# Layer norm centring in two rounded passes, with ScalarE's half copies one step earlier

## The reference

```
for i in range(6):
    x = attention(shift_tokens(x)) + x      # 16 heads of 64, windows of 32 with the window before
    x = ffn(shift_tokens(x)) + x

shift_tokens(t): the first 64 channels as they are, the last 64 one token later (zero first)
attention: q, k, v = t @ Wqkv; q, k L2-normalised, scaled, rotated; softmax(8 q k') v; @ Wo
ffn: mu = mean(t); var = mean((t - mu)^2)
     xn = (t - mu) / sqrt(var + 1e-5) * g + b
     a, gate = split(xn @ W1 + b1); out = (a * gelu(gate)) @ W2 + b2
```

## Time and profile before

| | |
|---|---|
| median of 3 runs | 1684.48 us (1683.54 to 1689.99) |
| the profiled execution | 1684.45 us, its span 1682.7 us |
| PE busy | 1569.3 us (93%) |
| DVE busy | 1448.3 us (86%) |
| ACT busy | 1116.0 us (66%) |
| POOL busy | 1071.4 us (64%) |

### The profile page before, as it was taken

How to read it: one execution, slowest core, us unless ns; L and a number is a source line. 1 busy time by engine, 2 the same in 40 slices (tenths; PEclk the granted TensorE clock), 3 DMA queues, 4 the chain that set the end, 5 groups by cost and what they waited for, 6 DMA issues and landing times.

```text
span 1682.7 us, 77735 instructions
## 1 busy us (share of the span) xinstructions
PE 1569.3 (93%) x33167; PEld 1272.7 (76%) x33168; DVE 1448.3 (86%) x3173; ACT 1116.0 (66%) x2014; POOL 1071.4 (64%) x1040
## 2 busy tenths in 40 slices
PE   4469999999999999999999999999999999999987
PEld 2247878778878878888878787778788878887874
DVE  8969989889889988889988889889899888888862
ACT  4336677667677667677667676767766766776753
POOL 4656767675676666667667567576577585675640
PEclk7679999999999999999999999999999999999999
DMA  2011111211111211111211111211111111111010
GB/s 88 32 55 41 41 38 43 74 35 40 36 47 38 60 44 49 33 51 29 69 33 51 42 38 41 63 37 53 42 38 41 56 44 49 30 45 53 25 47 14
DMA packets 41086, 75.09 MB, mean 45 GB/s; under 512 B 9472, under 2 KB 22568, under 8 KB 40744
## 3 DMA queue, kind: packets, MB, share of 16 engines
q1 hardware_dynamic: 40744, 70.12, 14.4%
HBM read 20.08 MB, written 2.10 MB: 13 GB/s over the span
## 4 chain that ended last, share of the span: by engine, by line
PE 72%; issue 8%; DVE 7%; ACT 4%; POOL 4%; ACTq 0%; DVEq 0%; POOLq 0%
PE bank L1372 8%; PE bank L1340 8%; PE bank L1423 7%; PE bank L1497 7%; PE wide L1465 7%; PE bank L1342 6%; PE bank L1341 6%; PE bank L1482 5%; PE bank L1562 4%; PE bank L1442 3%; PE bank L1411 2%; PE bank L1547 2%; POOL qk L864 2%; PE bank L1548 1%; PE bank L1549 1%
## 5 line engine op out<-in xcount | busy, mean ns | idle before, releaser
L872 POOL TENSOR_TENSOR qk<-qk,rnorm 128x512 f32<-128x512 f32 x384 | 402.2, 1048 | 346.9 <-DVE rnorm L1025 346.9
L864 POOL TENSOR_TENSOR qk<-qk,qk_sin 128x512 f32<-128x512 f32 x384 | 492.7, 1283 | 144.3 <-DVE qk_sin L986 144.3
L1188 ACT ACTIVATE squares<-bank 128x512 f32<-128x512 f32 x384 | 229.7, 598 | 152.2 <-DVE qk_sin L986 152.2
L996 DVE TENSOR_REDUCE norm<-squares 128x8 f32<-128x512 f32 x384 | 258.0, 677 | 30.7 <-ACT squares L1188 28.5
L1340 PE MATMUL bank<-w_hi,xs_hi 128*128 128x512 f32 x576 | 263.3, 457 | 11.8 <-ACT squares L1188 6.6
L979 DVE TENSOR_TENSOR qk<-bank,tables 128x512 f32<-128x512 f32 x384 | 261.2, 680 | 7.3 <-PE bank L1342 7.1
L986 DVE TENSOR_TENSOR qk_sin<-bank,tables 128x512 f32<-128x512 f32 x384 | 260.8, 679 | 0.6 <-POOL qk L864 0.6
L1372 PE MATMUL bank<-ident,qk 128*128 128x128 f32 x1536 | 225.2, 277 | 4.9 <-POOL qk L872 4.1
L1342 PE MATMUL bank<-w_hi,xs_lo 128*128 128x512 f32 x576 | 228.2, 396 | 0.0
L1341 PE MATMUL bank<-w_lo,xs_hi 128*128 128x512 f32 x576 | 227.2, 394 | 0.7 <-issue 0.7
L1372 PEld LDWEIGHTS bank<-ident,qk 128*128 128x128 f32 x1536 | 180.5, 141 | 42.7 <-POOL qk L872 4.9
(11 more groups left out here) (181 smaller groups left out, 2738.7 us busy)
## 6 DMA issues: line engine op xcount, KB each, us to landing
v<-v SPq DMA_DIRECT2D x96, 390.0 KB, 3.5
v<-v SPq DMA_DIRECT2D x72, 130.0 KB, 3.5
w_raw<-in_L_ffn_Wqkv SPq DMA_DIRECT2D x36, 256.0 KB, 3.1
w_o_s<-in_L_ffn_Wo SPq DMA_DIRECT2D x6, 512.0 KB, 4.0
w_raw<-in_L_ffn_W SPq DMA_DIRECT2D x6, 341.0 KB, 3.4
mix_x_nat<-in_L_attn_x SPq DMA_DIRECT2D x4, 256.0 KB, 3.2
w_raw<-x_res_scratch SPq DMA_DIRECT2D x4, 256.0 KB, 3.3
out<-w_raw SPq DMA_DIRECT2D x4, 256.0 KB, 3.1
```

Source lines behind the costliest of these rows:

```text
L864: pool.tensor_tensor(qk[:, g % 2, c, :], qk[:, g % 2, c, :], qk_sin[:, (QK_CHUNKS * g + c) % SINES, :], ALU.add).then_inc(added[c], 1)
L872: pool.tensor_tensor(view, view, rnorm[:, g % 2, c * HPC:(c + 1) * HPC].unsqueeze(2) .to_broadcast([P, HPC, DH]), ALU.mult).then_inc(norme ...
L996: dve.tensor_reduce(norm2[:, c * HPC:(c + 1) * HPC], squares[:, c % 2, :].rearrange("p (h d) -> p h d", d=DH), AX.X, ALU.add).then_inc(sum ...
```

## The change

`centre` becomes two passes with rounded operands: `center_r` times `xs2_hi`, and later `center_r` times `xs2_lo`, summed in bank 5. `center_r` is a rounded copy of `center`, made once by DVE. `xs2_hi` is made by ACT (`round_tail`), `xs2_lo` by POOL (`split_tail`); they use the memory of `xn_hi` and `xn_lo`. The half copies leave the start of `t == 3`: the first (`take_tail`) stands in step `t == 2` behind `take_probs`, the second (`shift_tail`) in the same step behind `square(step, 3)`. `lo_ready` takes the place of `xn_ready` and counts both low parts. Three small tensors of the root become slices of one.

```
@@ constants and tensors
-    N_CONST = 9
+    N_CONST = 10
-        norm2, root_t, root_w = (sb(name, [P, NORMS + NBLK]) for name in ("norm2", "root_t", "root_w"))
+        norms = sb("norms", [P, 3, NORMS + NBLK])
+        norm2, root_t, root_w = (norms[:, n, :] for n in range(3))
+        xs2_hi, xs2_lo = xn_hi, xn_lo
+        center_r = sb("center_r", [P, P], F32R)
-        xn_ready, gelu_done = sem("xn_ready"), sem("gelu_done")
+        lo_ready, gelu_done = sem("lo_ready"), sem("gelu_done")
@@ POOL
             def split_xn(m):
-                ....then_inc(xn_ready, 1)
+                ....then_inc(lo_ready, 1)
+            def split_tail(m):
+                if not real(m):
+                    return
+                pool.wait_ge(xs2_ready, 3 * (m + 1))
+                pool.tensor_tensor(xs2_lo[:], xs2[:], xs2_hi[:].bitcast(F32), ALU.subtract).then_inc(lo_ready, 1)
             def add_first_residual(m):
-                pool.wait_ge(xs2_ready, 2 * (m + 1))
+                pool.wait_ge(xs2_ready, 3 * (m + 1))
@@ POOL, in each step
+                if t == 3:
+                    split_tail(item - 1)
                 normalise(step - 1, 3)
                 add(step - 1, 2)
@@ DVE, once
+            dve.tensor_scalar(center_r[:], center[:], 1.0, 0.0, ALU.mult, ALU.add).then_inc(constants_ready, 1)
             dve.wait_ge(constants_ready, N_CONST)
@@ ACT
+            def take_tail(m):
+                if not real(m):
+                    return
+                act.wait_ge(x1_done, NBLK * (m + 1))
+                need(act, lo_ready, 2 * m - 1)
+                act.copy(xs2[0:half, :], x1[0:half, m % 2, :]).then_inc(xs2_ready, 1)
             def shift_tail(m):
-                act.wait_ge(x1_done, NBLK * (m + 1))
-                need(act, centred, m)
-                act.copy(xs2[0:half, :], x1[0:half, m % 2, :]).then_inc(xs2_ready, 1)
                 act.copy(xs2[half:P, 1:SEQ], x1[half:P, m % 2, 0:SEQ - 1]).then_inc(xs2_ready, 1)
+            def round_tail(m):
+                if not real(m):
+                    return
+                act.wait_ge(xs2_ready, 3 * m + 2)
+                need(act, up_ready, NHID * m)
+                act.copy(xs2_hi[:], xs2[:]).then_inc(xs2_ready, 1)
@@ ACT, in each step
                 if t == 3:
-                    shift_tail(item - 1)
+                    round_tail(item - 1)
                 take_v(step, 0)
                 take_qk(step - 2, 0)
@@
                 take_probs(step - 2, 0)
                 take_probs(step - 2, 1)
                 if t == 2:
+                    take_tail(item - 1)
                     take_out(item - 2)
                 if t == 0:
                     gelu(item - 2, 0)
                 square(step, 3)
+                if t == 2:
+                    shift_tail(item - 1)
                 take_qk(step - 1, 2)
                 take_v(step, 1)
@@ PE
             def centre(m):
-                pe.wait_ge(xs2_ready, 2 * (m + 1))
+                pe.wait_ge(xs2_ready, 3 * (m + 1))
-                pe.matmul(bank[5][:], center[:], xs2[:], start=True, stop=True).then_inc(centred, 1)
+                pe.matmul(bank[5][:], center_r[:], xs2_hi[:], start=True, stop=False)
+            def centre_rest(m):
+                if not real(m):
+                    return
+                pe.wait_ge(lo_ready, 2 * m + 1)
+                pe.matmul(bank[5][:], center_r[:], xs2_lo[:], start=False, stop=True).then_inc(centred, 1)
             def expand(m, j):
-                    pe.wait_ge(xn_ready, m + 1)
+                    pe.wait_ge(lo_ready, 2 * m + 2)
@@ PE, in each step
                 weigh(step - 3, 1)
+                if t == 3:
+                    centre_rest(item - 1)
```

More of the change, by code:

```diff
@@ L878, in split_xn @@
                 pool.wait_ge(xn_copied, 2 * (m + 1))
-                pool.tensor_tensor(xn_lo[:], xn[:], xn_hi[:].bitcast(F32), ALU.subtract).then_inc(xn_ready, 1)
+                pool.tensor_tensor(xn_lo[:], xn[:], xn_hi[:].bitcast(F32), ALU.subtract).then_inc(lo_ready, 1)
+            def split_tail(m):
[3 more added lines that the diff above has]
+                pool.tensor_tensor(xs2_lo[:], xs2[:], xs2_hi[:].bitcast(F32), ALU.subtract).then_inc(lo_ready, 1)
             def add_first_residual(m):
```

## The result

| | before | after |
|---|---|---|
| median (4 runs each) | 1685.8 us (1683.54 to 1689.99) | 1714.35 us (1704.67 to 1717.62) |
| ratio, with 95% interval | | 1.0158 [1.0136, 1.0181] |
| profiled execution, its span | 1684.45 us, 1682.7 us | 1716.12 us, 1714.3 us |

The kernel became 1.6% slower. The forecast was 1704 us with a range of 1682 to 1711, so the direction was right and the time lies 3 us above the range. The two profiled executions differ by 31.7 us; the sum had 19.4.

A forecast was written before the change was run, and what follows sets the result against it. The prediction took PE (93% busy) as the bound. Ordinary items 5.2, items 4n + 3 6.5, items 4n + 2 6.3, last item 1.2 and rounding `center` 0.2 sum to 19.4 us on 1684.48: 1704 us, range 1682 to 1711.

The forecast's parts named there:

- PE's saving: Centring on PE: two rounded passes instead of one fp32 product save 0.39 us per item, 9.4 us for 24.
- The stall of the k copy: Inside PE's eight transposes of t = 3: the k copy, delayed by `shift_tail`, stalls PE 0.57 us per item.
- PE's own 0.18: PE's net loss per item, the stall beyond the 0.39 us saved; claimed hidden beside the late root's 0.40 us.
- a tie, at most 0.1: `take_centred` would end at about 835.4, just when `score` wants it, costing at most 0.1 us.
- ordinary items: 13 items where the root, held by POOL's `split_tail`, comes 1.3 us late: 0.40 us each, 5.2 us.
- The 0.90: Root lateness taken as hidden, read from a root 1.09 us late with `merge_heads` only 0.19 late.
- Items 4n + 2: In five layers `split_tail` directly follows the weight split and holds the root another 1.28 us: 5 x 1.25 = 6.3 us.
- Items 4n + 3: In five layers POOL's `normalise` starts 1.3 us late and all of it reaches PE: 5 x 1.3 = 6.5 us.
- an end: The last item, with nothing beside the chain: rounding and low part come in, PE's saving goes: 1.2 us.
- Rival A: At the root: POOL does not hold it up, PE's balance alone decides, 5.5 us lost, 1690 us; chance 0.20.
- Rival B: At the shared port: the root keeps POOL out, so the low part comes late; 22 us, 1707 us; chance 0.12.
- Rival C: On PE: the 0.39 us saving per item survives, k copy delay under 0.58 us; 1675 us; chance 0.13.

The follow-up runs named there:

- e1: Kernel before with only ScalarE's two half copies moved into step t = 2, centring still one fp32 product: 1697.72 us, 1.0082.
- e3: Kernel after with the second half copy (`shift_tail`) moved behind the two copies PE waits for: 1707.43 us, 1.0145 of the kernel before.
- e6: Kernel before with one more GpSimd tensor_tensor of 128x512, which reads SBUF, put beside the root: 1692.3 us, 1.005.
- e7: Kernel before with a GpSimd memset of 128x512, which only writes, put beside the root: 1686.74 us, 1.0003.
- e0_after: Kernel after run once more, unaltered, in five rounds: 1717.09 us, 1.0187 of the kernel before.
- e2: Kernel after without the low part: no `split_tail` and no second centring pass: 1699.61 us, 1.0094 of the kernel before.
- e4: Kernel after with the low part computed by DVE behind the root instead of by POOL: 1712.0 us, 1.0152 of the kernel before.
- e9: Kernel after without the low part, a narrow matmul replacing each pass left out, and `shift_tail` late: 1682.65 us, 0.9975 of the kernel before.
- e8: Kernel after without the low part, a narrow matmul replacing each pass left out to keep PE's program length: 1697.3 us, 1.0062 of the kernel before.
- e5: Kernel after with the low part on DVE behind the root and `shift_tail` late: 1705.02 us, 1.011 of the kernel before.
- e10: Kernel after with six small matmuls put into PE's wait that opens a layer: 1717.85 us, 1.0188 of the kernel before.

## Why the forecast was wrong

- **PE's saving: right.** From the start of the centring to the second pass of the next projection it was 832.16 to 834.24 and is 916.49 to 918.17: 2.08 and 1.68 us, 0.40 less where the forecast had 0.39. The row of the kernel before at which the stretch ends:

```profile
834.24 0.39 PE L1341 MATMUL bank<-w_lo,xs_hi 128*128 128x512 f32 x1
```

- **The stall of the k copy: mechanism right, 0.57 was too little.** It is 0.74 (e1). The delay of the copy was nearly right, 1.27 us behind the square for 0.49, so 0.78 for 0.75 (the square itself is not late: the first transpose starts 0.79 behind it in both kernels). The slack was wrong. The forecast took the 0.19 us from the end of the k copy to the fifth transpose as free. Wherever PE waits for this copy, its transpose starts 0.14 after the copy's end, so some 0.06 was free. The idle time of 0.54 in the row looks like the 0.57, but it is counted from the modelled end of the fourth transpose; from start to start the fifth comes 0.72 later, and the end of the eight 0.74.
- **"PE's own 0.18 runs beside it and is covered by it": this step failed.** The balance of PE is 0.74 - 0.40 and 0.10 more, for which `score` waits for `take_centred` (L1437 above starts 0.63 behind the first product of `turn_o`, and 0.53 in the kernel before); the forecast called this "a tie, at most 0.1" and left it out of the balance. That is 0.44, not 0.18, and it is the larger of the two in ordinary items. The root is 1.04 late, not 1.3, and the kernel covers 0.74 of it, not 0.90; that leaves 0.30, not 0.40. The 0.90 came from items 4n + 2 of the kernel before, read from the centring to `merge_heads` (0.19 late); from one residual addition to the next these items are 0.35 longer than the others, which is 1.09 less 0.74. So the k copy and the wait for `take_centred` set the ordinary items and the root is hidden under them: the reverse of the forecast. That the floor came out near the forecast term (0.45 for 0.40) is luck. e3 removes the stall and gains little, since the root then takes its place.
- **Items 4n + 2: right.** 1.03 for 1.25; the two held instructions are in the trace.
- **Items 4n + 3: half.** 0.45 + 0.23 = 0.68 for 1.3; POOL's queue was 0.5 us later at PE, since part of the root's delay falls into time in which PE was late itself.
- **The sum over these items was 18.0 us and 18.9 were measured** (17.7 and 1.2). This too is luck: the 13 ordinary ones took 10.0 for 5.2, with the further gaps in them, items 4n + 2 5.1 for 6.3, and items 4n + 3 3.7 for 6.5. What put the time outside the range is, beside that, what the sum hadn't: three drops of the clock (5.1 us in the profiled execution; over the whole span the time at half speed rose from 71.8 to 91.2 us, which bounds the cost at 9.7), 5.3 us more of gaps in PE's small matmuls, in part within the 10.0, and an end of 2.4 us where 1.2 was forecast. The range had no term for either of the first two, though the time in the earlier trace rows under "issue", 8% of the chain, was there to be asked about. The range's upper end was no sum of its own bounds either: 13 x 0.7 + 5 x 1.4 + 5 x 1.3 + 1.4 is 24.0 us, which gives 1708 and not 1711.
- **The rule of the Trainium skill** in SBUF — State Buffer, section "Who interferes with whom", that a two-input VectorE instruction excludes a GpSimd instruction that reads SBUF and not one that only writes it, is what the runs show: L1034 took 1.23 beside L888, L1031 0.92 beside e6's reading instruction and 0.19 beside e7's memset. Rival A, the free root, is out by that. Rival B, the root keeping POOL out, is out too: L888 takes its 1.29 whole. Rival C, faster, needed the k copy less than 0.58 late; it was 0.78.

What stays open: why the clock drops after the same 1.84 us gap in some executions and not in others. Of the five openings of a layer it did so at two in the kernel after, at three in e0_after, at one each in e2, e3, e4 and e9, at two in e8 and at none in e5. But it also did so in kernels whose centring is the old one: at three in e1, at three in e6, at one in e7, at none in the kernel before. That is 11 of 40 against 7 of 20, so nothing here shows that the change brings these drops about. The lower mean clock of the kernel after (0.973 against 0.978) is not explained. Also open is how much of e2's and e10's extra gaps would stay if the program were shifted by another few matmuls; that wasn't tried.

## What to carry to other kernels

Before an instruction is moved in front of another on a filled engine, find the consumer of the one behind it and its slack: 0.06 us of slack against 0.78 of delay cost more here than the two passes save. A distance between two rows is slack only after the time that the signal takes (0.14 of the 0.19 us here). Where two delays run side by side, price each against its own slack and take the larger, and test by removing each alone, since removing one shows the other. A gain of some tenths per item on an engine with ten thousands of instructions is of the size by which a changed program length alone moves the time (e2: 14.5 us), so a padded twin belongs beside each such experiment.

## What the runs showed of the hardware

- The port shared by DVE and POOL goes to whoever comes first, for a whole instruction, in both directions: 32-column instructions of 0.19 us took 1.23 behind a 1.29 us subtraction, and POOL's 1.04 took 1.43 behind DVE's 0.69.
- A memset of POOL on its own (0.53 us) held none of the root's two-input instructions, but where it followed the weight split directly, the tensor_scalar L1027 was held through both, 1.73 us.
- ACT: two instructions that read PSUM start 0.49 us apart; where a half copy from SBUF to SBUF stands before or behind, it is 0.63 to 0.65 (square to half copy 0.63, half copy to k copy 0.64, two half copies 0.65).
- PE loses 0.1 to 2.5 us at some points of a long run of small matmuls, at distances that are multiples of some 125 records, and which points do is a matter of the place in the program: 27 to 49 such gaps with 20 to 36 us in the twelve kernels. All but one in each trace end 1.2 to 1.6 us after a 16 KB packet of the queue "instruction" has ended.
- The granted clock can fall to 1.2 GHz for 3.4 us right after PE stood still for 1.8 us or more between busy stretches; of the eighteen steps that open a layer with such a drop, seventeen are 1.3 to 1.7 us longer than in the kernel before. Between 130 and 1640 us of the thirteen traces there are 24 drops and 65 gaps of that length, and 23 of the drops stand behind one. With the gap cut to 0.5 us or less none came in the five places of e10.
- PE starts 0.14 us after the end of the k copy, a copy of ScalarE, where it waits for it.
